# In-place low half of the residual on GpSimd, another order of SP's transfers, and the first norm and the clears moved, in a fused attention and feed-forward kernel

## The chip, the cores and the metric

One core of one Trainium2 chip. The metric is the device time of one execution in microseconds; it is given as the median of three runs. The core has five engines with instruction streams of their own, tied by semaphores: TensorE (PE), VectorE (DVE), ScalarE (ACT), GpSimd (POOL) and SyncE (SP), which here only issues DMA transfers.

## What is computed

A transformer layer on 2048 tokens of width 1024. The attention mixes the 32 heads of one token with each other (not tokens with tokens); the feed-forward weights are first quantized to 16 levels per block of 64 values and back.

```python
def reference(x, wq, bq, wk, bk, wv, bv, wl, bl, w1, w2, w3):
    x = x + attn(layernorm(x))
    x = x + ffn(layernorm(x))
    return x

def attn(h):                                  # heads H = 32, head width D = 32
    q, k, v = ((h @ w.T + b).reshape(B, S, H, D) for w, b in ...)
    scores = einsum("bshd,bstd->bsht", q, k) / sqrt(D)
    return einsum("bsht,bstd->bshd", softmax(scores), v).reshape(B, S, E)

def ffn(h):                                   # w1, w2: 2752 x 1024, w3: 1024 x 2752
    dq = nf4_quant_dequant                    # per block of 64: nearest of 16 levels times the block's absmax
    return (silu(h @ dq(w1).T) * (h @ dq(w2).T)) @ dq(w3).T
```

## The kernel before

Everything that PE multiplies in 16 bits is split into a high half (the value rounded to float16) and a low half (the rest), and the products are added.

**Stages.** The program first turns and splits the three projection weights (to about 64 us). Then comes the attention stage, 16 steps, one for each tile of 128 tokens: steps 0 and 1 are written out (`first_steps`), steps 2 to 13 are a loop of six passes with two steps each (u = 0, the even step, and u = 1), and steps 14 and 15 are written out. A short tail finishes the last two tiles while the first feed-forward weights are prepared. Then 11 rounds of feed-forward.

**One step n on PE** (`tensor.step`): the q projection of tile n (L1014), mixed with the scores of tile n-1 (L1051); the transposes of the normed tile n+1 (L285), which need DVE's norm L279; the k projection, mixed with the first half of the context products of tile n-1 (L1063), and the v projection with the second half. The context products need `p_diag`, written by ACT (L933).

**DVE in step n** (`vector.step`): evacuates projections (L752), takes norm statistics of tile n+1 (L261, L265, L267), applies the norm once POOL has the reciprocal root (L275), handles scores and softmax, and in between does four or five "looks" (L766): each takes block maxima of one tile of a feed-forward weight, which SP has loaded into one of two slots of `ff_raw`. A look waits for its load; a load waits until an earlier look has freed its slot.

**The second residual stream** (called with n-2): POOL adds the context to `x_res` (`residual`, L715); SP stores the sum as x1 (`store_x1`, L655); DVE takes its moments and normalizes `x_res` in place (L879) after that store; ACT writes the high half into `x2_half` (`halve2`, L981) and issues a DMA transpose of it to `x2_hi` (L609); POOL computes the low half into `x2_half` again (`low2`, L723), for which it waits until the high transpose has landed; ACT issues the transpose of it to `x2_lo` (L614) after `q_diag` (L933) is dispatched; SP stores both (`store_x2`, L661) and loads the next tile's residual into `x_res` (`load_res`, L256). In the tail SP issues the transposes itself. In the rows digits are left out of names: `x_half` is `x2_half`, `x_lo` is `x2_lo`, `x` as a target of L655 is x1.

**Order.** Each engine executes its stream in the order in which the step functions emit it, so SP, which waits on a semaphore before most transfers, holds back all transfers behind a wait. POOL clears `q_diag` and `p_diag` by one memset each in steps 0 and 1 (`clear`, L739).

## Time and profile before

| | us |
|---|---|
| median of 3 runs | 2000.74 |
| lowest and highest | 1997.92, 2001.58 |
| the profiled execution | 2001.23 |
| its span | 1999.5 |
| PE busy in the span | 1916.9 (96%) |
| DVE busy | 1740.5 (87%) |
| ACT busy | 1479.4 (74%) |
| POOL busy | 1192.9 (60%) |

The durations further down come from that one profiled execution, whose own time is 0.5 us above the median. Shares over the whole span mix stages: the attention stage fills about 64 to 580 us, the feed-forward rounds the rest. Times of a row are microseconds from the start of the span. Busy time of a matmul is modelled, so PE counts as busy where matmuls follow each other without a gap.

### The profile page before, as it was taken

What the parts mean: (1) busy time and instruction counts of PE and PEld (TensorE: products, weight loads), DVE (VectorE), ACT (ScalarE), POOL (GpSimd) and SP (SyncE); (2) the same over time, 40 slices, a digit from 0 to 9 for tenths busy, and PEclk for the clock granted to TensorE, in tenths of its full rate; (3) what the DMA queues carried; (4) which work ended last, traced back from release to release, by engine and by line L of the source; (5) the groups of instructions that cost most, each with busy time, mean ns of one, the idle gap of its engine ahead of it and who ended that gap; (6) DMA issues with size and microseconds to landing.
All of it is one profiled execution on the core that took longest, in us unless ns stands there. A gap on an engine that the chain in (4) does not pass through costs nothing. (4 is left out here: it accounts for less than half of the span.)

```text
span 1999.5 us, 31160 instructions
## 1 busy us (share of the span) xinstructions
PE 1916.9 (96%) x10444; PEld 1061.6 (53%) x10444; DVE 1740.5 (87%) x1853; ACT 1479.4 (74%) x1672; POOL 1192.9 (60%) x715
## 2 busy tenths in 40 slices
PE   6799999999988989999999999999999999999998
PEld 5487787777764334444444444444444444444443
DVE  6687878788777899999989999899998989999982
ACT  7234334352466889989989899898998989998883
POOL 0112121111143778787787977879778797786975
PEclk9899999999999999999999999999999999999999
DMA  9225554545345732221222212122121221212114
GB/s 305 95 85 147 161 165 131 183 129 178 108 169 132 231 91 53 53 54 42 56 50 48 57 42 62 44 53 53 42 63 43 57 49 42 63 42 59 38 27 180
DMA packets 253838, 184.06 MB, mean 92 GB/s; under 512 B 177840, under 2 KB 220848, under 8 KB 253744
## 3 DMA queue, kind: packets, MB, share of 16 engines
q1 hardware_dynamic: 224176, 175.67, 31.0%
q10 hardware_dynamic: 29568, 7.34, 1.9%
q8 instruction: 34, 0.56, 0.1%
q14 instruction: 60, 0.49, 0.1%
HBM read 115.34 MB, written 25.17 MB: 70 GB/s over the span
## 5 line engine op out<-in xcount | busy, mean ns | idle before, releaser
L1491 ACT ACTIVATE signs<-w_nat,compare_bias 128x1024 int8<-128x1024 f32 (+2 forms) x896 | 959.1, 1132 | 21.9 <-issue 14.5
L1627 DVE SCALAR_TENSOR_TENSOR bank<-signs,bank 128x1024 f32<-128x1024 int8 (+2 forms) x761 | 926.6, 1218 | 48.5 <-ACT signs L1491 20.8
L1798 PE MATMUL bank<-x2T_hi,w12T_hi 128*128 128x512 f16 x1376 | 522.6, 380 | 10.6 <-DMA w12T_lo<-half 6.4
L1800 PE MATMUL bank<-x2T_hi,w12T_lo 128*128 128x512 f16 x1376 | 522.5, 380 | 0.0
L1799 PE MATMUL bank<-x2T_lo,w12T_hi 128*128 128x512 f16 x1376 | 522.5, 380 | 0.0
L1014 PE MATMUL bank<-wT_hi,xT_hi 128*128 128x512 f16 x768 | 294.0, 383 | 2.4 <-PEq L325 2.4
L1014 PE MATMUL bank<-wT_hi,xT_lo 128*128 128x512 f16 x768 | 293.8, 383 | 0.0
L1825 PE MATMUL bank<-w3T_hi,hT_hi 128*128 128x512 f16 x672 | 255.7, 380 | 9.3 <-DMA w3T_lo<-half 3.8
L1827 PE MATMUL bank<-w3T_hi,hT_lo 128*128 128x512 f16 x672 | 255.6, 380 | 0.0
L1826 PE MATMUL bank<-w3T_lo,hT_hi 128*128 128x512 f16 x672 | 255.4, 380 | 0.0
L1417 POOL TENSOR_TENSOR acc<-acc,hidden 128x512 f32<-128x512 f32 x176 | 221.1, 1271 | 34.6 <-ACT hidden L1540 33.8
L1384 POOL TENSOR_SCALAR step_part<-w_nat 128x1024 f32<-128x1024 f32 (+1 forms) x64 | 230.5, 3602 | 14.3 <-POOL w_nat L1397 7.4
L1798 PEld LDWEIGHTS bank<-x2T_hi,w12T_hi 128*128 128x128 f16 x1376 | 134.6, 98 | 174.9 <-issue 6.4
L1800 PEld LDWEIGHTS bank<-x2T_hi,w12T_lo 128*128 128x128 f16 x1376 | 134.7, 98 | 162.8 <-issue 0.8
L1799 PEld LDWEIGHTS bank<-x2T_lo,w12T_hi 128*128 128x128 f16 x1376 | 134.7, 98 | 162.4 <-issue 0.8
L1393 POOL TENSOR_TENSOR w_nat<-w_nat,step_part 128x1024 f32<-128x1024 f32 (+1 forms) x64 | 149.8, 2340 | 101.6 <-DVE w_nat L1627 101.6
L966 ACT ACTIVATE probs<-probs 128x512 f32<-128x512 f32 x32 | 20.2, 631 | 238.3 <-DVE probs L873 238.0
L1540 ACT ACTIVATE hidden<-bank,un_scale 128x512 f32<-128x512 f32 x176 | 120.2, 683 | 91.5 <-PE bank L1827 36.1
L1063 PEld LDWEIGHTS bank<-vT,p_diag 128*128 128x128 f32 x1024 | 168.8, 191 | 22.4 <-ACT p_diag L933 7.8
L1051 PEld LDWEIGHTS bank<-kT,q_diag 128*128 128x128 f32 x1024 | 169.1, 191 | 14.6
L1063 PE MATMUL bank<-vT,p_diag 128*128 128x32 f32 x1024 | 155.9, 235 | 4.8 <-ACT p_diag L933 4.8
L1411 POOL TENSOR_TENSOR hT_lo<-hidden,hT_hi 128x512 f16<-128x512 f32 (+1 forms) x88 | 101.8, 1157 | 95.5 <-ACT hT_hi L1529 92.8
(143 smaller groups left out, 2613.7 us busy)
## 6 DMA issues: line engine op xcount, KB each, us to landing
ff_raw<-in_L_ffn_w SPq DMA_DIRECT2D x63, 512.0 KB, 5.1
w_nat<-in_L_ffn_w SPq DMA_DIRECT2D x63, 512.0 KB, 3.9
x_nat<-in_L_attn_hidden_states SPq DMA_DIRECT2D x16, 512.0 KB, 4.6
x_res<-in_L_attn_hidden_states SPq DMA_DIRECT2D x16, 512.0 KB, 4.0
x<-x_res SPq DMA_DIRECT2D x16, 512.0 KB, 3.1
acc<-x SPq DMA_DIRECT2D x4, 2048.0 KB, 8.5
out<-acc SPq DMA_DIRECT2D x16, 512.0 KB, 2.7
w_raw<-in_L_attn_wq SPq DMA_DIRECT2D x8, 512.0 KB, 7.4
```

The source lines that it names most:

```text
L1014: ins = nc.tensor.matmul(to, x, w, start=j == 0, stop=j == len(passes) - 1)
L1063: ins = nc.tensor.matmul(context[:, t], p_diag[:, t], vT[:, t // 2, :, t % 2], start=True, stop=True)
L1384: nc.gpsimd.tensor_scalar(step_part[0:rows, 0:cols], w_nat[0:rows, slot, 0:cols], float(BOUNDS[APART]), 2 * HALF_STEP[APART], ALU.is_gt, A ...
L1417: nc.gpsimd.tensor_tensor(acc[:, st, BANK:], acc[:, st, BANK:], hidden[:, st % 2], ALU.add).then_inc(summed, 1)
L1491: nc.scalar.activation(signs[0:rows, ring(v, k), 0:cols], w_nat[0:rows, v % SLOTS, 0:cols], ACT.Sign, scale=COMPARE[SUMMED[k]][0], bias=co ...
L1627: V.scalar_tensor_tensor(to, part, HALF_STEP[SUMMED[k]], before, ALU.mult, ALU.add).then_inc(sign_used, 1)
L1798: nc.tensor.matmul(dst, hi, x2T_hi[:, toks, c], start=c == 0, stop=False)
L1799: nc.tensor.matmul(dst, hi, x2T_lo[:, toks, c], start=False, stop=False)
L1800: last = nc.tensor.matmul(dst, lo, x2T_hi[:, toks, c], start=False, stop=c == C - 1)
L1825: nc.tensor.matmul(dst, hT_hi[k, p, toks], w3T_hi[k, p, cols], start=p == 0, stop=False)
L1826: nc.tensor.matmul(dst, hT_hi[k, p, toks], w3T_lo[k, p, cols], start=False, stop=False)
L1827: last = nc.tensor.matmul(dst, hT_lo[k, p, toks], w3T_hi[k, p, cols], start=False, stop=p == GROUP - 1)
```

## The change

Six edits:

1. `low2` writes the low half into the first half of `x_res`'s own bytes, seen as float16 (`x2_low`), instead of into `x2_half`. It waits for the high half (`x2_hi_done`), no longer for the high transpose. The low transpose reads `x2_low`.
2. ACT issues the low transpose before it places `q_diag`, no longer after.
3. SP's order within a step is another, and `load_res` waits for both transposes, since `x_res` now holds the low half until it is turned. In the tail SP issues the low transpose first and loads `x_res` when it has landed.
4. In the first step DVE takes the norm statistics before the first look, and applies the norm before the first evacuation and look.
5. POOL clears both `diag` tiles before the first step instead of in steps 0 and 1.
6. The first `load_res` and what stands behind it no longer wait for the first projection.

```diff
+        x2_low = x_res[:].bitcast(F16)[:, 0:E]
...
         def turn_low2(eng, n):
             eng.wait_ge(x2_lo_done, n + 1)
             eng.sem_inc(held, 1)
-            eng.dma_start_transpose(x2_lo[:], x2_half[:]).then_inc(x2_turned, 16)
+            eng.dma_start_transpose(x2_lo[:], x2_low).then_inc(x2_turned, 16)
...
                 todo = looks(n, u, it)
-                for look in todo[:1]:
+                for look in todo[:2]:
                     load_ff(*look)
                 if end:
                     store_x1(n - 2)
+                for look in todo[2:3]:
+                    load_ff(*look)
                 if normalize and not (it is None and n + 2 >= T):
                     sp.wait_ge(x_turned, 2 * n + 2)
                     load_x(sp, n + 2, u)
...
-                for look in todo[1:4]:
+                for look in todo[3:4]:
                     load_ff(*look)
                 if end:
                     sp.wait_ge(x2_turned, 32 * (n - 1))
-                    store_x2(n - 2)
+                    sp.sem_inc(held, 1)
+                for look in todo[4:]:
+                    load_ff(*look)
                 if end and attend:
                     load_res(sp, n - 1)
+                if end:
+                    store_x2(n - 2)
...
-                for look in todo[4:]:
-                    load_ff(*look)
...
                 turn_high2(sp, T - 2)
-                sp.wait_ge(x2_lo_done, T - 1)
+                turn_low2(sp, T - 2)
+                sp.wait_ge(x2_turned, 32 * (T - 1))
+                sp.sem_inc(held, 1)
                 load_res(sp, T - 1)
-                turn_low2(sp, T - 2)
                 store_x2(T - 2)
...
-            sp.wait_ge(projected, 1)
+            sp.wait_ge(w_turned, GROUPS * PAIRS)
             load_res(sp, 0)
...
             def low2(n):
-                pool.wait_ge(x2_turned, 32 * n + 16)
-                nc.gpsimd.tensor_tensor(x2_half[:], x_res[:], x2_half[:], ALU.subtract).then_inc(x2_lo_done, 1)
+                pool.wait_ge(x2_hi_done, n + 1)
+                nc.gpsimd.tensor_tensor(x2_low, x_res[:], x2_half[:], ALU.subtract).then_inc(x2_lo_done, 1)
...
+            pool.wait_ge(w_turned, GROUPS * PAIRS)
+            for diag in (q_diag, p_diag):
+                pool.memset(diag[:], 0.0).then_inc(diag_zero, 1)
             all_steps(pool, step, tail, feed)
...
                     turn_v(n)
-                look()
+                    look()
...
+                if normalize and not attend:
+                    norm_apply(dve, n + 1, 1 - u)
+                    look()
                 if project:
                     evacuate(n, u, it, 0, 0)
                 if attend:
                     center(n, 0)
-                if normalize:
+                if normalize and attend:
                     norm_apply(dve, n + 1, 1 - u)
...
                 if feed:
                     next(feed)
+                if end:
+                    turn_low2(act, n - 2)
                 if project:
                     act.wait_ge(q_ready, n + 1)
...
                     place(q_diag, qT[:].rearrange("p t h u -> p t u h"), q_placed)
-                if end:
-                    turn_low2(act, n - 2)
```

DVE at the start of the attention stage, before (`ff_raw` is the look's tile, `x_nat` the tile to be normed):

```order
L766 TENSOR_REDUCE absmax<-ff_raw 128x16 [waits bias_turned,ff_in0,bias_in,consts_set]
L261 BN_STATS stats<-x_nat 128x6 [waits x_in1]
L261 BN_STATS stats<-x_nat 128x6
L265 BN_AGGR mean_var<-stats 128x2 [waits dve_seq]
L267 TENSOR_SCALAR var_eps<-mean_var 128x1 [waits dve_seq]
L752 SCALAR_TENSOR_TENSOR qkv<-bank,scales,bias 128x512 [waits projected]
L279 TENSOR_SCALAR x_nat<-x_nat,mean_var,rstd 128x1024 [waits rstd_ready]
```

DVE at the same place now:

```order
L261 BN_STATS stats<-x_nat 128x6 [waits bias_turned,x_in1,bias_in,consts_set]
L261 BN_STATS stats<-x_nat 128x6
L265 BN_AGGR mean_var<-stats 128x2 [waits dve_seq]
L267 TENSOR_SCALAR var_eps<-mean_var 128x1 [waits dve_seq]
L279 TENSOR_SCALAR x_nat<-x_nat,mean_var,rstd 128x1024 [waits rstd_ready]
L769 TENSOR_REDUCE absmax<-ff_raw 128x16 [waits ff_in0]
L755 SCALAR_TENSOR_TENSOR qkv<-bank,scales,bias 128x512 [waits projected]
```

The first look moved from ahead of the statistics to behind the norm, and the norm from behind the first evacuation to ahead of it.

SP in the second half of the loop's even step, before, from the fourth look's load to the fifth's (a wait is named at the instruction behind it; the ISA and REGISTER_ALU rows prepare an address):

```order
L625 DMA ff_raw<-in_L_ffn_w 128x8x128
L643 REGISTER_ALU
L661 REGISTER_ALU [waits x2_turned]
L661 DMA x_hi_dram<-x_hi 128x1024
L661 DMA x_lo_dram<-x_lo 128x1024
L256 ISA
L256 DMA x_res<-in_L_attn_hidden_states 128x1024
L619 REGISTER_ALU
L623 ISA [waits absmax_done]
L623 DMA ff_raw<-in_L_ffn_w 128x1024
```

SP at the same place now:

```order
L626 DMA ff_raw<-in_L_ffn_w 128x8x128
L646 REGISTER_ALU
L620 REGISTER_ALU [waits x2_turned]
L624 ISA [waits absmax_done]
L624 DMA ff_raw<-in_L_ffn_w 128x1024
L256 ISA
L256 DMA x_res<-in_L_attn_hidden_states 128x1024
L666 REGISTER_ALU [waits x2_turned]
L666 DMA x_hi_dram<-x_hi 128x1024
L666 DMA x_lo_dram<-x_lo 128x1024
```

The fifth look's load moved ahead of the load of `x_res` and the two stores, and the load of `x_res` ahead of the stores.

SP in the tail, before, around the last load of `x_res`:

```order
L609 DMA_TRANSPOSE x_hi<-x_half 128x8x128 [waits x2_out,x2_hi_done]
L256 DMA x_res<-in_L_attn_hidden_states 128x1024 [waits x2_lo_done]
L614 DMA_TRANSPOSE x_lo<-x_half 128x8x128 [waits x2_lo_done]
L661 DMA x_hi_dram<-x_hi 128x1024 [waits x2_turned]
L661 DMA x_lo_dram<-x_lo 128x1024
```

SP at the same place now:

```order
L610 DMA_TRANSPOSE x_hi<-x_half 128x8x128 [waits x2_out,x2_hi_done]
L615 DMA_TRANSPOSE x_lo<-x_res 128x8x128 [waits x2_lo_done]
L256 DMA x_res<-in_L_attn_hidden_states 128x1024 [waits x2_turned]
L666 DMA x_hi_dram<-x_hi 128x1024 [waits x2_turned]
L666 DMA x_lo_dram<-x_lo 128x1024
```

The load of `x_res` moved behind the low transpose, and waits for it.

## Rows read from the trace of the kernel before

**Rows 1.** Table by stretches: busy us of PE, its weight loads, DVE, ACT, POOL.

```profile
1000.00:1500.00 500.00, 499.89 (x2315) 225.83 (x2313) 470.67 (x435) 451.48 (x492) 401.17 (x218) 1.00 0.22 51
```

**Rows 2.** Waits of PE, 60:130 us, then 130:600: total us, times, longest.

```profile
PE bank L285 <- DVE x_nat L279: 9.7, 1, 9.7
...
PE bank L285 <- DVE x_nat L279: 10.2, 7, 2.4
...
PE bank L1063 <- ACT p_diag L933: 4.8, 7, 0.8
```

**Rows 3.** Timelines at the start: start, duration, instruction, [idle before, what ended it].

```profile
71.06 0.37 SPq L623 DMA_DIRECT2D ff_raw<-in_L_ffn_w  x1
...
76.10 1.22 DVE L766 TENSOR_REDUCE absmax<-ff_raw 128x16 f32<-128x1024 f32 x1 [11.87 <-DMA ff_raw<-in_L_ffn_w]
...
79.64 3.52 POOL L739 MEMSET q_diag<- 128x4096 f32 x1
...
79.73 3.97 DVE L279 TENSOR_SCALAR x_nat<-x_nat,mean_var,rstd 128x1024 f32<-128x1024 f32 x1
...
83.76 1.97 PE L285 MATMUL bank<-ident,x_nat 128*128 128x128 f32 x8 [9.71 <-DVE x_nat L279]
```

**Rows 4.** Table by stretches: after the busy times granted clock, DMA share, GB/s.

```profile
84.00:89.00 5.00, 5.00 (x17) 2.73 (x17) 4.79 (x6) 1.93 (x3) 0.00 (x0) 0.50 0.34 107
```

**Rows 5.** Timelines of one odd step of the loop.

```profile
304.17 0.80 DVE L279 TENSOR_SCALAR x_nat<-x_nat,mean_var,rstd 128x1024 f32<-128x1024 f32 x1
...
305.02 1.09 PE L285 MATMUL bank<-ident,x_nat 128*128 128x128 f32 x8 [1.88 <-DVE x_nat L279]
...
311.04 1.04 ACT L981 ACTIVATE x_half<-x_res 128x1024 f16<-128x1024 f32 x1
...
315.32 2.13 POOL L723 TENSOR_TENSOR x_half<-x_res,x_half 128x1024 f16<-128x1024 f32 x1 [12.46 <-DMA x_hi<-x_half]
...
316.16 0.41 PE L1063 MATMUL bank<-vT,p_diag 128*128 128x32 f32 x2 [0.66 <-ACT p_diag L933]
...
317.57 1.25 ACTq L614 DMA_TRANSPOSE x_lo<-x_half  x1
318.44 2.29 ACT L933 ACTIVATE q_diag<-qT 32x1024 f32<-32x1024 f32 x2
...
325.41 0.75 DVE L752 SCALAR_TENSOR_TENSOR qkv<-bank,scales,bias 128x512 f32<-128x512 f32 x1 [0.96 <-PE bank L1014]
```

**Rows 6.** Timelines at the end of the even step that follows.

```profile
354.09 1.25 DVE L855 STREAM_TRANSPOSE flipped<-probs 128x1024 f32<-128x1024 f32 x1
358.63 1.22 DVE L766 TENSOR_REDUCE absmax<-ff_raw 128x1024 f32 x1 [3.29 <-DMA ff_raw<-in_L_ffn_w]
...
351.71 0.36 SPq L661 DMA_DIRECT2D x_hi_dram<-x_hi  x1
...
353.38 0.86 SPq L623 DMA_DIRECT2D ff_raw<-in_L_ffn_w  x2
```

**Rows 7.** Timelines of the tail and the opening of the feed-forward rounds.

```profile
625.93 0.33 SPq L256 DMA_DIRECT2D x_res<-in_L_attn_hidden_states  x1
...
630.72 0.35 SPq L661 DMA_DIRECT2D x_hi_dram<-x_hi  x1
...
632.69 0.59 SPq L655 DMA_DIRECT2D x<-x_res  x1
...
629.84 2.39 POOL L715 TENSOR_TENSOR x_res<-x_res,flipped 128x1024 f32<-128x1024 f32 x1 [2.08 <-DMA x_res<-in_L_attn_hidden_states]
...
642.08 0.81 DVE L879 TENSOR_SCALAR x_res<-x_res,mean_var,rstd 128x1024 f32<-128x1024 f32 x1 [6.83 <-DMA x<-x_res]
...
647.79 2.13 POOL L723 TENSOR_TENSOR x_half<-x_res,x_half 128x1024 f16<-128x1024 f32 x1 [12.95 <-DMA x_hi<-x_half]
...
654.24 1.06 ACT L1514 ACTIVATE half<-w_nat 128x1024 f16<-128x1024 f32 x1 [5.14 <-POOL w_nat L1397]
...
656.37 9.23 DVE L1627 SCALAR_TENSOR_TENSOR bank<-signs,bank 128x1024 f32<-128x1024 int8 x7 [2.56 <-ACT signs L1491]
```

More of the change, by code:

```diff
@@ L699, in step @@
                     inv_std(pool, n + 1)
-                if it is None:
-                    clear(n)
                 if end:
@@ L735, in tail @@
                 low2(T - 1)
-            def clear(n):
-                if n < 2:
-                    pool.memset((q_diag, p_diag)[n][:], 0.0).then_inc(diag_zero, 1)
+            pool.wait_ge(w_turned, GROUPS * PAIRS)
+            for diag in (q_diag, p_diag):
+                pool.memset(diag[:], 0.0).then_inc(diag_zero, 1)
             all_steps(pool, step, tail, feed)
```

## The prediction

> **What bounds the kernel now.** I read the table by stretches first. In the long feed-forward stretch TensorE (PE) is busy 499.9 of 500 us [rows 1]. Nothing of the change lies there, so whatever the attention stage gains or loses before about 740 us is passed on whole to the end. Next the waits of PE in the attention stage: one of 9.7 us at its start, seven of 10.2 us together for `x_nat` (L285), and seven of 4.8 us together for `p_diag` (L1063) [rows 2]. All of these are waits for VectorE (DVE) or for ScalarE (ACT) behind it. The timelines then say what held those engines. Reader, look at the square brackets: the idle time of the engine before the row, and what ended it.
>
> **Start of attention, the first norm ahead of the looks, the early clears.** DVE sat idle 11.87 us until `ff_raw` landed for the first look at 76.10; SP had issued that load only at 71.06, because it first waited for the first projection [rows 3]. The norm statistics of tile 1 stood behind that look although their data was there. Then the norm itself (L279) took 3.97 us, where the same instruction takes 0.80 later [rows 3, 5]: it ran beside the 3.52 us memset of GpSimd (POOL) and ended half a microsecond after it (79.64 + 3.52 = 83.16 against 83.70). PE had been ready at 83.76 - 9.71 = 74.05.
> In the changed order DVE starts with the statistics. The stage begins between 64.23 (76.10 - 11.87, where DVE was done with the stage before) and 65.3 (I take 64.4). POOL is the later one: two memsets, 7.0 us, then the reciprocal root, about 0.6 with its gap: 72.0, at latest 73.0. The norm's 0.80 ends at 72.9, at latest 73.8. Both are ahead of 74.05, so the whole wait goes: **9.7 us**. What is late next is PE itself, by a margin of 0.25 to 1.2 us.
> The gap also cost clock. After it PE ran 84 to 89 us at a granted clock of 0.50, that is at 1.2 instead of 2.4 GHz [rows 4]; from 83.76 to 89 that is 5.2 us of which half is lost, **2.6 us**. An idle of 1.88 us at 305 was followed by eight transposes in 1.09 us, where those after the long idle took 1.97 [rows 3, 5], so short waits do not bring this cost and only the long one does.
> The Trainium skill (SBUF — State Buffer, on the port pair shared by VectorE and GpSimd) calls the pair an exclusive lock for a whole instruction, taken by a VectorE instruction in a two-port mode. The trace agrees: 3.97 against 0.80 us. By this rule the statistics, with one input each, are not held up by the two memsets; if the small L267 were, it would still be free at the end of the first one, near 68, before POOL can use it.
>
> **SP's transfers by date; low half in place.** One step per token tile, two tiles per pass of the loop. In the odd step of a pass the norm starts at 304.17, PE had waited 1.88 us for it at 305.02, and it waits again 0.66 us for `p_diag` at 316.16 [rows 5]. Both hang on the same DVE chain, so the step loses 2.54 us. What made DVE late is at the end of the even step: its fifth look began 3.29 us late, waiting for `ff_raw` [rows 6]. DVE was through with `flipped` at 354.09 + 1.25 = 355.34, but SP issued that load (the first of the two at 353.38) behind the two stores of x2 and the load of `x_res`, and those stood behind the low transpose.
> Two edits bring it forward. First, the low half: ACT has written `x2_half` at 311.04 + 1.04 = 312.08, but POOL starts only at 315.32, when the high transpose has landed, and the low transpose is issued at 317.57, behind the dispatch of `q_diag` [rows 5]. Now POOL can run at 312.1 to 314.3. ACT's queue reaches the transpose when `p_diag` is nearly done, 314.8 to 316.1, so it goes out and lands 1.5 to 2.8 us earlier. Second, SP issues the fifth load directly after it instead of behind three other transfers (351.71 to 353.38, 1.7 us more). Together the load leaves 3.2 to 4.5 us earlier and lands, with the same 5.2 us of flight, at 354.1 to 355.4, as DVE gets there. Of the 3.29 us at most 0.1 stays; PE needs 2.54, so 0.65 us or more is spare. Both waits of PE go: 7 places, 10.2 + 4.8 = **15.0 us** [rows 2].
> What the edits cost there: the same transfers, the same POOL subtraction (2.13 us, nobody waits for POOL at 312). ACT now issues the low transpose (1.25 us of its queue) ahead of `q_diag`, which can begin up to 1.3 us later. It ended at 318.44 + 2.29 = 320.73; PE starts the next tile about 325.4 (DVE's row at 325.41 follows PE's last product) [rows 5], so 4.7 us of cover become 3.4. SP waits for x_res's store (residual) before the third look's load and the next `x_nat`; these are used 7 and 30 us later. The residual add itself may start earlier, since `x_res` is loaded ahead of the stores. I cost all of this at nothing.
>
> **Change to the tail.** The load of the last `x_res` was issued at 625.93, as soon as POOL had read it. Now the low half lives in `x_res`, so the load waits until the low transpose has landed, which was seen at 630.72 [rows 7]; without the load beside it I take 630. The last residual moves from 629.84 to about 634, and the store of x1 from 632.69 to about 637. That store, not the add, holds DVE: it landed when norm L879 could start at 642.08, 9.4 us after its issue, because token loads of 2 MB stood in front. They still do. Two halves of x2, 2 MB of tokens and this store, 3 MB, passed between 630.72 and 642.08, 0.26 MB/us. The 0.5 MB of `x_res` that now travel ahead in the same stretch make 1.9 us, less 0.7 for the stretch's earlier start: +1.2 us.
> Against it: POOL's last low half waited 12.95 us until 647.79 for the high transpose. Now it follows the half at 644 and frees POOL 2.6 us sooner, after which ACT's wait of 5.14 us (ended at 654.24) and the 2.56 us of DVE at 656.37 fall away [rows 7]. The chain of quantized weights through DVE sets PE's waits up to 740 us, so the tail gives 2.6 - 1.2 = **1.4 us**. Ends of this term: 3 us of cost, if the store lands 3 us later and nothing is given back, and 4 us of gain, if the store keeps its date and later waits of PE shrink too.
> The Trainium skill (DMA: Bandwidth & Descriptors, Queues, rings and completion order) says each DMA engine takes the descriptors of a ring in order. The 9.4 us of a 512 KB store agree. By this rule alone 512 KB put ahead are a loss of their whole passage, 1.9 in place of 1.2 us, and the sum is 0.7 us worse.
>
> **Sum.** 9.7 + 2.6 + 15.0 + 1.4 = 28.7 us. The profiled execution took 2001.2 us (its span 1999.5, and 1.7 around it), 0.5 above the median 2000.7. So 1972.5 for an execution like it, and **1972.0** as a median.
>
> **Rivals.**
> (a) The loop's wait is only passed on. If PE finds another limit in place of `x_nat` (the fifth load lands late in the burst of four transfers that now leave together, or `p_diag` keeps its own date), half or all of the 15 us stays. For it: the two waits of a step come in a row, and DMA is crowded there. Against: the even steps have the same chain and no wait at all, with DVE 3.3 us better off. Times: 1979.5 with half, 1987 with all.
> (b) The tail costs. The last x_res load is late, the 2.56 us are not given back and the store lands 3 us later: 1.4 + 3 = 4.4 us more, 1976.4.
> (c) Slower. GpSimd's in-place write of a 16-bit tile over the 32-bit one that it reads is a form that no row has. The nearest (L723, in place in 16 bits) takes 2.13 us. If it took D us, `q_diag` would end at 312.1 + D + 1.25 + 4.6, and PE's scores wait from D = 7.5 us on, 14 times. The gain of 28.7 us is used up 2.05 us further, at D = 9.5. At D = 10.5 it costs 14 x 3 = 42 us: 2014. Nothing speaks for a factor of five.
> (d) The change does not do what it says at the start: POOL's memsets begin late and the norm misses 74.05. Up to 2 us are lost, without a fall of the clock: 1974, inside the forecast's own spread.
>
> **Chances.** Forecast with (d): 0.62. (a): half 0.11, all 0.07. (b): 0.13. (c) 0.03, and 0.04 for a result within 0.2% by several of these at once. A measurement of this kernel tells about 0.2%, 4 us, from no change. Faster by more: 0.93; within: 0.04; slower: 0.03. The range reaches down to 1966.5 (the tail's 4 us instead of 1.4, and 3 more if DVE's shorter waits bring PE forward elsewhere too) and up to 1983, which takes in (b), half of (a) and both at once; about 0.15 is left out.
>
> **What would show it.** In the profile after: the wait before the first L285 of the attention stage under 1 us, L279 there near 0.8 us, and no stretch at clock 0.50 near 84 us. The seven waits for `x_nat` and seven for `p_diag` gone, and DVE's wait for `ff_raw`, now up to 3.29 us at a time, under 0.5 us in the loop. POOL's low half right behind ACT's half. In the tail, norm L879 0 to 2 us later against its neighbours, POOL's last low half at once. Wrong it would be if PE waits in the loop under another name, or if the last `x_res` moves PE's first waits in the feed-forward part by more than 3 us.

## The result and the profile after

| | before | after |
|---|---|---|
| median, us | 1999.99 | 1967.39 |
| lowest and highest, us | 1997.92, 2001.58 | 1964.42, 1968.27 |
| span of the profiled execution, us | 1999.5 | 1966.5 |

The ratio of after to before is 0.9835, 95% interval 0.9818 to 0.9852. By the medians the kernel is 32.6 us faster, by the spans 33.0; the forecast was 28.7. The median of before is 1999.99 and not 2000.74, because a fourth run of it was taken beside the changed kernel. Of the runs further down, one of the eight executions of e9_slow1 took 6561.78 us and is left out of that kernel's ratio. In the code of after most line numbers are 2 to 6 higher (L1014 is L1020, L1063 is L1069, L879 is L885, L723 is L727, L766 is L769), and the in-place low half shows as `x_res<-x_res,x_half` in the rows.

The start of attention, timelines of all engines, in the columns of [rows 3]:

```profile
68.12 3.51 POOL L743 MEMSET p_diag<- 128x4096 f32 x1
71.60 0.56 POOL L275 TENSOR_TENSOR rstd<-var_eps,power 128x1 f32<-128x1 f32 x1
72.20 0.81 DVE L279 TENSOR_SCALAR x_nat<-x_nat,mean_var,rstd 128x1024 f32<-128x1024 f32 x1 [5.38 <-POOL rstd L275]
...
74.05 1.04 PE L285 MATMUL bank<-ident,x_nat 128*128 128x128 f32 x8
```

The norm ends at 73.01 and PE does not wait. The row of the table by stretches that answers to [rows 4]:

```profile
84.00:89.00 5.00, 5.00 (x26) 2.38 (x25) 2.10 (x4) 0.00 (x0) 0.00 (x0) 1.00 0.39 105
```

The granted clock is 1.00 where it was 0.50, and PE runs 26 instructions in the 5 us where it ran 17. The waits of PE in 130:600 us, all there are (against the lower two of [rows 2]; the 9.0 us stood there in the trace of before too):

```profile
PE bank L1861 <- issue: 9.0, 1, 9.0
PE bank L1804 <- DVE w_nat L1650: 2.6, 1, 2.6
PE bank L1861 <- ACT hT_lo L1508: 0.9, 1, 0.9
```

**Where the 33.0 us lie.** The first transposes of `x_nat` of each step (L285) are good dates, since each step has them once. Three of before, then three of after:

```profile
143.22 1.07 PE L285 MATMUL bank<-ident,x_nat 128*128 128x128 f32 x8
...
176.40 1.09 PE L285 MATMUL bank<-ident,x_nat 128*128 128x128 f32 x8 [2.38 <-DVE x_nat L279]
...
208.00 1.07 PE L285 MATMUL bank<-ident,x_nat 128*128 128x128 f32 x8
```

```profile
130.78 1.07 PE L285 MATMUL bank<-ident,x_nat 128*128 128x128 f32 x8
...
161.43 1.07 PE L285 MATMUL bank<-ident,x_nat 128*128 128x128 f32 x8
...
192.07 1.07 PE L285 MATMUL bank<-ident,x_nat 128*128 128x128 f32 x8
```

Behind a first one of 30.64 us the period was 32.0 to 33.2 us in one step and 31.6 (32.0 in the last) in the next, in turn; it is 30.64 in every step now. Summed up from such dates:

| stretch | before | after | gain | forecast |
|---|---|---|---|---|
| wait before the first L285 | 9.71 | 0 | 9.7 | 9.7 |
| first to second L285 | 28.82 | 26.09 | 2.7 | 2.6 |
| second to last L285 (13 steps) | 416.12 | 398.36 | 17.8 | 15.0, with the next line |
| last L285 to the first L1855 (now L1861) | 59.40 | 58.16 | 1.2 | |
| behind it, to the end | | | 1.6 | 1.4 |

Of the 4.3 us that came beyond the forecast, 4.0 are the loop's (17.8 and 1.2 against 15.0).

### The profile page after: what moved, and what is told of

Its sections match the earlier page's. It is cut to its first block and busy times, and to the rows that moved or that the text cites. A ratio compares the mean times of both kernels' runs of the same rounds, so it can differ in the third digit from the quotient of the medians.

```text
span 1966.5 us, 31163 instructions
## 1 busy us (share of the span) xinstructions
PE 1910.7 (97%) x10444; PEld 1060.9 (54%) x10444; DVE 1734.3 (88%) x1853; ACT 1479.7 (75%) x1672; POOL 1193.6 (61%) x715
## 5 line engine op out<-in xcount | busy, mean ns | idle before, releaser
L1804 PE MATMUL bank<-x2T_hi,w12T_hi 128*128 128x512 f16 x1376 | 522.2, 379 | 8.1 <-DMA w12T_lo<-half 5.5
L1020 PE MATMUL bank<-wT_hi,xT_hi 128*128 128x512 f16 x768 | 292.6, 381 | 2.4 <-PEq L325 2.4
L1020 PE MATMUL bank<-wT_hi,xT_lo 128*128 128x512 f16 x768 | 292.6, 381 | 0.0
L1804 PEld LDWEIGHTS bank<-x2T_hi,w12T_hi 128*128 128x128 f16 x1376 | 134.8, 98 | 172.0 <-issue 4.2
L972 ACT ACTIVATE probs<-probs 128x512 f32<-128x512 f32 x32 | 20.2, 630 | 217.7 <-DVE probs L879 217.3
L1069 PEld LDWEIGHTS bank<-vT,p_diag 128*128 128x128 f32 x1024 | 169.0, 191 | 14.8
L1410 POOL TENSOR_TENSOR half<-w_nat,half 128x1024 f16<-128x1024 f32 (+1 forms) x66 | 139.8, 2118 | 31.9 <-ACT half L1520 31.9
```

The costliest lines, as they stand in the source:

```text
L1020: ins = nc.tensor.matmul(to, x, w, start=j == 0, stop=j == len(passes) - 1)
L1804: nc.tensor.matmul(dst, hi, x2T_hi[:, toks, c], start=c == 0, stop=False)
```

## A wait costs more than its row says

Here is why, in rows of before around one wait for `p_diag` in an odd step (first fence) and at the same place in the even step that follows (second):

```profile
186.13 0.38 PE L1014 MATMUL bank<-wT_hi,xT_lo 128*128 128x512 f16 x1
186.35 0.30 PE L1063 MATMUL bank<-vT,p_diag 128*128 128x32 f32 x2
186.49 0.38 PE L1014 MATMUL bank<-wT_hi,xT_hi 128*128 128x512 f16 x1
187.54 0.41 PE L1063 MATMUL bank<-vT,p_diag 128*128 128x32 f32 x2 [0.67 <-ACT p_diag L933]
187.78 0.38 PE L1014 MATMUL bank<-wT_hi,xT_lo 128*128 128x512 f16 x1
```

```profile
218.07 0.38 PE L1014 MATMUL bank<-wT_hi,xT_hi 128*128 128x512 f16 x1
218.43 0.41 PE L1063 MATMUL bank<-vT,p_diag 128*128 128x32 f32 x2
218.67 0.38 PE L1014 MATMUL bank<-wT_hi,xT_lo 128*128 128x512 f16 x1
```

Without a wait L1063 starts 0.22 us behind L1014 (186.13 to 186.35), although L1014's row lasts 0.38: matmuls overlap. At the wait it starts 1.05 behind (186.49 to 187.54), and the next L1014 follows after 0.24 in place of 0.14. The step loses 0.83 + 0.10 = 0.93 us where the bracket says 0.67, for the bracket counts from the modelled end of the product before. In the even step there is no bracket at all, and still 0.36 in place of 0.22 and 0.24 in place of 0.14: 0.24 us lost. Such a stall without a row stands in three of the six even steps (at 218.43, 282.52 and 347.06: 0.24, 0.18 and 0.24 us); at 155 us and in the last two there is none. For L285 the same correction is 0.15 us (33.18 - 30.64 = 2.54 for a bracket of 2.38 and no other wait). So: 10.2 + 7 x 0.15 for L285, 4.8 + 7 x 0.27 for `p_diag` in odd steps, and 0.7 in the three even ones: 18.6 us by an estimate from these rows, against 19.0 measured.

## The experiments

Each ratio is taken against runs of the kernel before on the same chip, so the ratios compare better than the medians. "Step 1" is first to second L285, "13 steps" second to last.

| kernel | median | ratio and interval | step 1 | 13 steps |
|---|---|---|---|---|
| after | 1967.39 | 0.9835 (0.9818 to 0.9852) | 26.09 | 398.36 |
| e1_start_only | 1986.45 | 0.9942 (0.9927 to 0.9957) | 26.10 | 413.47 |
| e2_no_start | 1978.69 | 0.9908 (0.9894 to 0.9921) | 28.82 | 398.36 |
| e3_sp_old | 1966.18 | 0.9840 (0.9826 to 0.9853) | 26.10 | 398.36 |
| e4_low_old | 1985.10 | 0.9936 (0.9922 to 0.9949) | 26.10 | 414.19 |
| e5_act_old | 1964.72 | 0.9837 (0.9819 to 0.9854) | 26.09 | 398.37 |
| e6_clears_old | 1965.97 | 0.9845 (0.9828 to 0.9862) | 26.10 | 398.36 |
| e7_tail_low | 1966.17 | 0.9844 (0.9828 to 0.9860) | 26.15 | 398.36 |
| e8_memset1 | 1971.10, 1 run | | 27.83 | 398.36 |
| e8_memset2 | 1975.93, 1 run | | 28.18 | 398.36 |
| e9_slow1 | 1993.79 | 0.9980 (0.9969 to 0.9992) | 26.16 | 417.33 |
| e9_slow2 | 2047.86 | 1.0248 (1.0231 to 1.0265) | 26.10 | 456.09 |
| e10_slow_half | 1982.31 | 0.9922 (0.9906 to 0.9939) | 26.16 | 405.95 |

**Start and loop apart (e1, e2).** e1 is the kernel before with the edits at the start alone:

```diff
-            sp.wait_ge(projected, 1)
+            sp.wait_ge(w_turned, GROUPS * PAIRS)
...
+            for diag in (q_diag, p_diag):
+                pool.memset(diag[:], 0.0).then_inc(diag_zero, 1)
...
+                if normalize and not attend:
+                    norm_apply(dve, n + 1, 1 - u)
+                    look()
```

> The kernel before with the edits at the start alone: first norm ahead of the looks, both clears first, SP's early wait. Loop, low half and tail stay as before. Comparing the two traces, TensorE reached the first feed-forward matmul 31.4 us earlier, of which I had forecast 27.3. Theory A (the start gives what its rows say: a wait of 9.7 us and 2.7 us of halved clock): 12.4 us faster than before, about 1987.6, and the seven waits for x_nat and seven for p_diag stay at 10.2 and 4.8 us. Rival B (the 4 us that came beyond the forecast belong to the start, since everything behind it begins better placed): 16.5 us faster, about 1983.5. Rival C (loop waits grow when the loop starts earlier against SP's loads): under 10 us faster, above 1990.

e2 is the changed kernel with this same diff taken back.

> The changed kernel with the start as before: first look ahead of the statistics, clears in steps 0 and 1, SP behind the first projection. Theory A: the loop's edits are worth 19.0 us and not the 15.0 of the rows, because a wait in a row is counted from the modelled end of the product before it, while the products are issued closer than they last (0.14 to 0.22 us apart with 0.30 to 0.38 in the row), and because waits of 0.2 us in the even steps have no row. With 1.5 to 2 us of the tail: 12.4 us slower than the changed kernel, about 1979.8, the wait of 9.7 us and a stretch at clock 0.50 back, and no wait of TensorE in the loop. Rival B (the extra 4 us are the start's): 1983.5.

Waits of PE in 130:600 us, e1 and then e2:

```profile
PE bank L1855 <- issue: 8.3, 1, 8.3
PE bank L285 <- DVE x_nat L279: 8.2, 6, 1.5
PE bank L1063 <- ACT p_diag L933: 4.8, 7, 0.8
```

```profile
PE bank L1861 <- issue: 7.4, 1, 7.4
PE bank L1861 <- ACT hT_lo L1508: 0.9, 1, 0.9
```

e2 has 398.36 us in its 13 steps: the loop's gain of 17.8 us does not need the start. Its wait of 9.7 us and its step 1 of 28.82 us are back. That bears out theory A in the trace: 12.4 us are the start's, 19.0 the loop's. The medians are too wide to add to it (against the changed kernel's ratio, e2 is 14.6 us slower where 12.4 were expected, and e1 gains 11.6 us over before, each good to some 3 us). One thing was not expected: in e1 the loop's 13 steps shrank too, from 416.12 to 413.47, for which I followed no cause. With the loop's own edits in place these 2.65 us are part of the 17.8.

**Which edit makes the loop's gain (e3, e4, e5).** e3 puts SP's order within the step back:

```diff
-                for look in todo[:2]:
+                for look in todo[:1]:
...
-                for look in todo[3:4]:
+                for look in todo[1:4]:
                     load_ff(*look)
                 if end:
                     sp.wait_ge(x2_turned, 32 * (n - 1))
-                    sp.sem_inc(held, 1)
-                for look in todo[4:]:
-                    load_ff(*look)
+                    store_x2(n - 2)
                 if end and attend:
                     load_res(sp, n - 1)
-                if end:
-                    store_x2(n - 2)
...
+                for look in todo[4:]:
+                    load_ff(*look)
```

> The changed kernel with SP's order in the step as before: the fifth look's load behind the stores of x2 and the load of x_res. Low half in place, ACT's order and the start stay changed. As the prediction reads it, the early low half alone brings the load 1.5 to 2.8 us forward, VectorE was 3.29 us late, and TensorE feels it from 0.75 us of lateness: 0 to 1.0 us in each of 7 passes, so 1967 to 1974.5. Rival (from the trace of the changed kernel, where the fifth load leaves at 325.62 and lands some 3 us before its look at 333.03, and the norm behind it ends 1.8 us before TensorE wants it): behind three more transfers it still comes in time, no wait in the loop at all, 1967.4 within 0.1%.

e4 keeps SP's new order and takes back the date of the low half and ACT's order:

```diff
-                pool.wait_ge(x2_hi_done, n + 1)
+                pool.wait_ge(x2_turned, 32 * n + 16)
...
-                if end:
-                    turn_low2(act, n - 2)
                 if project:
...
                     place(q_diag, qT[:].rearrange("p t h u -> p t u h"), q_placed)
+                if end:
+                    turn_low2(act, n - 2)
```

> The changed kernel in which GpSimd's low half waits for the high transpose again and ACT issues the low transpose behind q_diag, as before. SP's new order and the start stay. As the prediction reads it, SP's order alone brings the fifth load 1.7 us forward of the 3.29 us that it was late: 1.6 us stay at VectorE, 0.85 us at TensorE, in 7 passes 6 us, about 1973.5, with L279 and p_diag waits named in the loop. Rival (slack of 4.8 us in the changed kernel against 4 us of delay): no wait of TensorE in the loop, 1967.4 within 0.1%, and the low half in place is then not needed beside SP's order.

e5 has only the second half of that diff.

> The changed kernel, with ACT issuing the low transpose behind q_diag again; GpSimd's low half stays in place and without the wait for the high transpose. With both undone (e4) the loop's 15 us of waits were back, so this run says which of the two carries the gain. Theory A (the low half's date carries it): ACT's queue reaches the transpose some 3 us later than the 291.6 of the changed kernel's step, against a slack of 4.8 us, so no wait of TensorE in the loop, period of a step 30.64 us, 1967 within 0.1%. Rival (ACT's order carries it): the transpose leaves behind q_diag whatever GpSimd does, VectorE waits 1 to 2 us for the fifth look, and half of the 19 us is back, about 1976.

e3 and e5 cannot be told from the changed kernel, to 0.01 us in the 13 steps and within the intervals in the medians. e4 is 20.2 us slower than the changed kernel by the ratios (17.1 by the spans), and no better than e1. Its waits in 130:600 us, PE's and the one of DVE's that matters:

```profile
PE bank L1069 <- ACT p_diag L939: 7.5, 12, 0.8
...
PE bank L285 <- DVE x_nat L279: 4.3, 7, 1.8
```

```profile
DVE absmax L769 <- DMA ff_raw<-in_L_ffn_w: 24.3, 15, 3.2
```

PE's waits are spread over more steps and most are smaller, but the 13 steps take as long as in e1. The trace says why SP's order did not help. In e1 it is above all the fifth look of the even steps that waits for its load, 2.9 to 3.3 us at a time. In e4 that wait is 0.8 us or less, but now the first look of the next step waits, 1.2 to 3.2 us in every step: its load stands behind that of `x_res` and the two stores of x2.

```profile
154.49 1.22 DVE L769 TENSOR_REDUCE absmax<-ff_raw 128x1024 f32 x1 [2.51 <-DMA ff_raw<-in_L_ffn_w]
```

So SP's order by itself brought nothing (414.19 us against 413.47 with the old one), and ACT's by itself is not needed (e5). With GpSimd's low half in place and without the wait for the high transpose, either of them can be undone at no cost. That edit carries the loop's gain as far as these runs go. Two combinations were not run: the low half alone, with the old orders of both SP and ACT, and the old wait with ACT's new order. Both rivals of e4's expectation fell: I had 6 us and nothing, it was 20.

**How much room the low half has (e9, e10).** The prediction priced a slow low half as rival (c): D is the time from ACT's half to GpSimd's, and nothing should happen below 7.5 us. e9 puts a multiplication of `x_res` by 1.0 ahead of the subtraction, with a reciprocal root that repeats `rstd2` (the values stay the same), once or twice; e10 only the root, four times:

```diff
+                nc.gpsimd.tensor_tensor(rstd2[:], var_eps2[:], power[:, 0:1], ALU.pow).then_inc(more, 1)
+                nc.gpsimd.tensor_scalar(x_res[:], x_res[:], 1.0, None, ALU.mult).then_inc(more, 1)
+                pool.wait_ge(more, n * 2 + 2)
                 nc.gpsimd.tensor_tensor(x2_low, x_res[:], x2_half[:], ALU.subtract).then_inc(x2_lo_done, 1)
```

> The changed kernel with a slower low half: GpSimd also multiplies x_res by 1.0 in place and takes the reciprocal root once more in between, so that the low half is ready about 6.6 us after ACT's half (D, 2.1 in the changed kernel). The prediction's rival (c) says that TensorE feels nothing below D = 7.5 us: 1967 within 0.1%. Rival reading: the fifth look's load waits for the low transpose and has 4.8 us of slack, which D = 6.6 nearly uses: 0 to 1 us in each of 7 passes, up to 1974.

> The same with the multiplication and the root twice: D about 11.1 us. By the prediction's rival (c), whose limit is q_diag's date for the scores of TensorE: 14 x (11.1 - 7.5) = 50 us slower than the changed kernel, 2017. By the date of q_diag in the trace of the changed kernel (scores start at 303.44, q_diag could start at 289.38 + D + 1.25 and takes 4.6): limit D = 8.2, 14 x 2.9 = 41 us, 2008. By the fifth look alone (limit D = 7.0, 7 passes): 29 us, 1996.

D is 2.2 us in the changed kernel. It came out at 5.6 us in e9_slow1 (the half ends at 297.25, the low half at 302.84), and this cost 29 us by the ratios (25.7 by the spans), all of the loop's gain and more. In e9_slow2 it came out at 9.0 us, not 11.1, and cost 83 us. Each of my limits was too generous. e10 was then to find the limit:

> The changed kernel with the reciprocal root taken four more times ahead of the low half: ready about 4.6 us after ACT's half in place of 2.1, so that the low transpose is issued about 10.1 us after TensorE's transposes of x_nat. That distance is 7.6 us in the changed kernel, 8.8 with ACT's old order (no cost), 12.8 with one multiplication more (27 us slower), 12.6 before the change. Theory A: everything that SP issues next stands behind the landing of this transpose, the next step's first look above all; its load had 5.2 us more delay than in the changed kernel and VectorE waited 2.1 us for it, so 3.1 us were spare, and a transpose up to 10.7 us behind costs nothing: 1967 within 0.1%, no wait of TensorE in the loop. Rival (the cost grows evenly from the date of the changed kernel or of ACT's old order): 8 to 13 us slower, 1975 to 1980.

Theory A fell again: e10 is 17 us slower than the changed kernel by the ratios and 12.6 by the spans (1979.1 against 1966.5), 7.6 of them in the 13 steps. The first disturbed step shows which transfer is the tight one. SP's queue and DVE in e10, then the same two places after:

```profile
143.92 0.33 SPq L625 DMA_DIRECT2D ff_raw<-in_L_ffn_w  x1
...
146.07 0.35 SPq L625 DMA_DIRECT2D ff_raw<-in_L_ffn_w  x1
...
153.93 1.22 DVE L778 TENSOR_REDUCE absmax<-ff_raw 128x1024 f32 x1 [1.99 <-DMA ff_raw<-in_L_ffn_w]
```

```profile
143.91 0.35 SPq L624 DMA_DIRECT2D ff_raw<-in_L_ffn_w  x1
...
152.21 1.18 DVE L769 TENSOR_REDUCE absmax<-ff_raw 128x1024 f32 x1
```

Behind the landing of the low transpose SP issues five transfers in a row, 2 MB: the fifth look's load, `x_res`, two stores of x2, and the first look's load of the next step. In e10 the last of them was issued at 146.07 and landed 7.7 us later, at 153.8; DVE had been ready 1.8 us before. In the changed kernel the same load was issued at 143.91 and landed 6.2 us later, at 150.1, and DVE took it at 152.21: 2.1 us to spare. Over the 13 steps the first look's load has 1.8 to 2.8 us to spare; e10's expectation had worked out 3.1 from the waits of e9_slow1. In e5, whose low transpose leaves 8.8 us behind L285, the same load landed at 151.7 and DVE took it at 151.87: 0.1 us to spare, at no cost. In e10 the transfer also took 1.5 us longer than in the changed kernel, and the next load (issued at 150.22) went out while it was still on its way; that the one slowed the other is not shown.

This also explains e3: the order among the five hardly changes when the fifth of them lands (at 150.5 in e3, whose first L285 comes 1.0 us later than in the changed kernel). But the old order leaves less room. The smallest that any look has in the 13 steps is 0.2 us in e3 and 1.8 us in the changed kernel.

From there the lateness feeds itself. DVE is late, so its norm of `x_res`, ACT's half and the transpose come later in the next step: ACT's half starts 4.3 us behind L285 in the changed kernel (288.26 against 284.00) and 5.8 in e10 (292.47 against 286.67), the low transpose leaves 11.7 behind L285 where 10.1 had been put in. Before the change it was 12.55 [rows 5], now 7.61. That e5 with 8.8 costs nothing and e10 with 10.1 does, places the limit between them, and by e5's 0.1 us close to e5.

Of e10's 12.6 us by the spans, 7.6 are in the 13 steps, 3.1 more in PE's wait ahead of the first feed-forward matmul (12.1 us against 9.0), 1.1 elsewhere between the last L285 and that matmul, and 1.2 behind it; the start gave 0.4 back. What set the parts outside the 13 steps is open.

**The start: clears and clock (e6, e8).** e6 puts the clears back behind the reciprocal root in steps 0 and 1:

```diff
-            for diag in (q_diag, p_diag):
-                pool.memset(diag[:], 0.0).then_inc(diag_zero, 1)
...
+                if it is None:
+                    clear(n)
```

> The changed kernel with GpSimd's two clears back in steps 0 and 1, behind the reciprocal root. The prediction let the norm wait for two memsets (7.0 us) and end at 72.9. Theory A: with the statistics first the root is done near 68.5, the norm then runs beside the memset and takes about 3.9 us again, to about 72.7, still before TensorE wants it at 74.05; the second memset has 3 us of cover in step 1. No wait, 1967 within 0.1%, and the early clears are worth nothing by themselves. Rival: norm and memset in step 1 delay the second norm past TensorE's date of 100.14 by up to 3 us: about 1970.

```profile
66.28 0.56 POOL L275 TENSOR_TENSOR rstd<-var_eps,power 128x1 f32<-128x1 f32 x1 [14.74 <-DVE var_eps L267]
66.78 3.52 POOL L745 MEMSET q_diag<- 128x4096 f32 x1
66.87 3.97 DVE L279 TENSOR_SCALAR x_nat<-x_nat,mean_var,rstd 128x1024 f32<-128x1024 f32 x1 [0.68 <-POOL rstd L275]
```

The norm took its 3.97 us beside the memset again, and ended at 70.84, still 2.6 us ahead of PE's L285 at 73.43 (in the changed kernel 1.0 us ahead). Theory A holds: the early clears bring nothing. That leaves the order of DVE (edit 4) and SP's earlier loads (edit 6), which no run parts. The trace speaks for DVE's order: statistics and norm wait for no transfer of this stretch, and the norm ends at 73.01 whatever `ff_raw` does. But the first look now stands ahead of the first evacuation, and its load was issued at 65.10 where before it was 71.06 [rows 3]; whether the 12.4 us need edit 6 as well is not shown. e8 puts one or two more memsets (3.5 us each) ahead of the two, to let PE idle for a time that I set:

```diff
+            for k in range(1):
+                pool.memset(q_diag[:], 0.0).then_inc(more, 1)
+                pool.wait_ge(more, k + 1)
             for diag in (q_diag, p_diag):
```

> The changed kernel with one more memset of q_diag (3.5 us) ahead of the two. The first norm then ends at about 76.5 and TensorE, ready at 74.05, idles 2.5 us. Theory A: as after the idles of 1.2 to 2.4 us in the loop before the change, the clock does not fall: the step behind it keeps its 26.1 us from first to second transposes of x_nat, and the cost is the wait alone. Rival: any idle at the start costs clock, the step is over 27 us.

> The same with two more memsets (7.0 us): TensorE idles about 6.0 us. The 9.7 us of before brought a granted clock of 0.50 for 5 us and a step of 28.8 in place of 26.1 us. Theory A: an idle of 6 us does the same, full price: 6.0 + 2.7 us. Rival A2: the price comes only with the longer idle, 6.0 us alone and a step of 26.1. Rival A3: in between, a clock partly lower, a price that grows with the idle.

L285 in e8_memset1, and in e8_memset2:

```profile
76.26 1.92 PE L285 MATMUL bank<-ident,x_nat 128*128 128x128 f32 x8 [2.40 <-DVE x_nat L279]
```

```profile
81.10 1.97 PE L285 MATMUL bank<-ident,x_nat 128*128 128x128 f32 x8 [5.09 <-DVE x_nat L279]
```

After an idle of 2.40 us the eight transposes took 1.92 us, against 1.04 without, and step 1 took 27.83 us, 1.7 longer. After 5.09 us it was 2.1 longer, after 9.71 us 2.7 [rows 3]. The granted clock accounts for all three. It was 0.50 from 76.4 to 79.8 us in e8_memset1, from 78.4 to 85.3 in e8_memset2 and from 79.0 to 89.2 before the change. Of these stretches 3.4, 4.2 and 5.4 us lie behind the start of L285 (76.26, 81.10, 83.76), and half of that was lost: 1.7, 2.1 and 2.7 us. So in these three the price is half of what is left of the slow stretch when PE resumes, and it rises less than the idle does. e8_memset2 went by A3. Each of the two is a single run.

Theory A of e8_memset1 is wrong, and with it a sentence of the prediction: an idle of 2.38 us at 176.40 in the kernel before cost no clock (its period is explained above to the last 0.15 us), one of 2.40 us at the start did. Nor does the loop protect from it. e9_slow2, whose steps have several waits each, fell to 0.50 for 3.4 us five times in its 13 steps. Two of its L285, after a wait of 1.76 us and after one of 3.14:

```profile
450.24 1.96 PE L285 MATMUL bank<-ident,x_nat 128*128 128x128 f32 x8 [1.76 <-DVE x_nat L279]
...
557.96 1.09 PE L285 MATMUL bank<-ident,x_nat 128*128 128x128 f32 x8 [3.14 <-DVE x_nat L279]
```

The shorter wait had the transposes run at half speed, the longer one did not. The length of the last idle alone does not tell, and neither does the place; what does is not shown by these runs.

**The tail (e7).** The low half of tile 14 goes to a free tile, so that `x_res` is loaded as early as before the change:

```diff
+        tail_low = ff_raw[:, 1].bitcast(F16)[:, 0:E]
...
-                turn_low2(sp, T - 2)
-                sp.wait_ge(x2_turned, 32 * (T - 1))
-                sp.sem_inc(held, 1)
+                sp.wait_ge(x2_lo_done, T - 1)
                 load_res(sp, T - 1)
+                turn_low2(sp, T - 2, tail_low)
```

> The changed kernel with the low half of tile 14 alone (the one of the tail) written into the second slot of ff_raw, whose last look is over, and transposed from there. x_res is free as soon as GpSimd has read it, and SP issues its last load ahead of the low transpose, as before the change: about 595.1 where the changed kernel issues it at 598.25. Theory A (what the trace of the changed kernel shows: the norm L885 behind the store of x1 came only 0.4 us late against TensorE's dates): nothing that a median can tell, the norm at most 0.4 us earlier, 1967. Rival (the prediction's term of 1.2 us, or its end of 3 us): norm and all behind it 1.2 to 3 us earlier, 1964.4 to 1966.2.

The changed kernel in the tail, then e7; the matmul row is a date common to both:

```profile
598.25 0.34 SPq L256 DMA_DIRECT2D x_res<-in_L_attn_hidden_states  x1
599.35 0.39 PE L1804 MATMUL bank<-x2T_hi,w12T_hi 128*128 128x512 f16 x1 [2.63 <-DVE w_nat L1650]
...
604.93 0.36 SPq L660 DMA_DIRECT2D x<-x_res  x1
...
611.00 0.81 DVE L885 TENSOR_SCALAR x_res<-x_res,mean_var,rstd 128x1024 f32<-128x1024 f32 x1 [3.08 <-DMA x<-x_res]
...
612.98 2.13 POOL L727 TENSOR_TENSOR x_res<-x_res,x_half 128x1024 f16<-128x1024 f32 x1 [5.47 <-ACT x_half L987]
```

```profile
593.01 0.33 SPq L256 DMA_DIRECT2D x_res<-in_L_attn_hidden_states  x1
...
597.32 0.39 PE L1804 MATMUL bank<-x2T_hi,w12T_hi 128*128 128x512 f16 x1 [2.63 <-DVE w_nat L1650]
...
599.82 0.57 SPq L661 DMA_DIRECT2D x<-x_res  x1
609.55 0.81 DVE L885 TENSOR_SCALAR x_res<-x_res,mean_var,rstd 128x1024 f32<-128x1024 f32 x1 [7.18 <-DMA x<-x_res]
```

Against L1804 e7 issues the load of `x_res` 3.2 us earlier and the store of x1 3.1 us earlier, and the norm still starts 0.6 us later (12.23 behind L1804 against 11.65). The store took 9.6 us to land in e7 and 6.0 in the changed kernel: what it gains in date it spends behind the token load issued ahead of it (`x2T_lo`, L1340). In both kernels it landed 1.3 to 1.4 us behind that load, and in the kernel before too, so the norm's date went with the token load and not with the store's own issue. Theory A holds in the main (the norm came 0.6 us later, where at most 0.4 earlier was expected), and the medians agree.

No kernel of these beats the changed one by more than its interval.

## Why the prediction was right, point by point

- **Total.** 1972.0 was forecast, 1967.4 measured, 4.6 us less and inside the range, but only 0.9 us above its lower end. The range reached so far down for a gain of 4 us in the tail and for shorter waits elsewhere. What used it up was mostly neither: the loop's waits were read too short. To that extent it was luck. The direction, the mechanism at the start and the waits that go in the loop hold.
- **First norm.** Forecast: POOL is the later one, L279 ends at 72.9. Measured 73.01. The wait of 9.7 us is gone whole.
- **Clock.** 2.6 us forecast, 2.7 measured (28.82 against 26.09). The size was right, as it was read from the slow stretch itself. The sentence that short waits do not bring this cost was wrong: 2.40 us brought 1.7 us of it (e8_memset1).
- **Early clears.** I let the gain rest on them without asking what the norm would do beside a memset at its new date. e6 shows that it is in time either way; they cost nothing and brought nothing.
- **Loop, 15.0 us.** Mis-sized: 19.0. The rows understate a wait by 0.15 and 0.27 us, and the sentence "the even steps have the same chain and no wait at all" missed 0.18 to 0.24 us in three of the six, which has no bracket. The size of DVE's own wait was read from one pass too: 3.29 us was not the longest, at 165.87 it was 4.18.
- **Loop, the two edits.** This step failed in its working. The low transpose was to land 1.5 to 2.8 us earlier and SP's order to bring 1.7 us more, and the two were added up against the 2.54 us. The low half does it with SP's old order (e3), and SP's order without the low half does nothing (e4): it moved the fifth look's load forward and left the next step's first load behind the others. The transpose now leaves 4.9 us earlier against L285 (12.55 to 7.61). 1.8 of these are lateness that had fed itself (ACT's half started 6.02 behind L285 [rows 5], now 4.26), 3.2 the edit.
- **`q_diag` later at no cost.** Holds: scores of PE show no wait for it.
- **Tail, 1.4 us.** 1.6 measured, by two errors that cancel only in part. The norm L885 came 0.4 us late against the first feed-forward matmul, not 1.2: it starts right behind the store, and the store landed right behind the token load ahead of it, whatever its own date (e7). PE's waits behind it shrank from 1.54, 3.24 and 3.19 us to none, 2.48 and 3.03, together 2.5 us, as the 2.6 had been read; 0.9 us of it was lost again. 0.55 lie between the first feed-forward matmul and the wait of 0.9 us behind it (27.08 us before, 27.63 after), and they are clock: behind that matmul the granted clock was 0.50 for 2.9 us before and for 4.0 after, and half of the difference is lost. The rest, along the rounds, is not explained.
- **Rivals.** (a) and (b) did not come. (c) had the right place and a wrong price: the limit is not 7.5 us of D, by `q_diag`, but under 4.7 (e10), by the first look's load at the end of SP's row of transfers. GpSimd's in-place write takes 2.13 us as before, and that alone kept (c) away. Had the low half come at D = 5.6 us, the kernel would have been nearly as slow as before (e9_slow1, 0.9980).

## What to carry to other kernels

Ask of an edit not only which wait it removes but by how much the new date is in time, at the last transfer of the burst that hangs on it, not at the first: here that transfer had 2 us to spare and not the 3 to 5 that I had worked out, and a low half 2.5 us later used them up. Read its landing in the trace of the kernel itself. A new order of transfers can buy room and no time: SP's left 1.8 us in place of 0.2, and no run here needed them. The wait in a row of overlapping matmuls was too small here each time (0.67 for 0.93 us, 2.38 for 2.54), and dates of one line from step to step give the true loss, small unnamed stalls included. When several edits come together, undo them one at a time: of six here, the low half without its wait carries the loop, and the edits of the start other than the clears carry the start; between DVE's order and SP's earlier loads these runs do not decide.

## What the runs showed that was not expected

- PE's idle of 2.40 us at the start cost 1.7 us of clock, 5.09 us cost 2.1 and 9.71 us 2.7. In the loop 2.38 us cost none before the change, but in e9_slow2 a wait of 1.76 us was followed by transposes at half speed and one of 3.14 us was not.
- A low half that came 2.5 us later on GpSimd cost 17 us, 3.4 us later cost 29 us: past the limit the loop loses in most steps, since the lateness comes round again through ACT's half.
- PE's wait ahead of the first feed-forward matmul, for which the profile names nothing, differs between kernels that are alike up to it: 9.0 us in the changed kernel, 7.6, 7.2, 7.9 and 7.2 in e3, e5, e6 and e7. That is of the size of the differences between their medians (1964.7 to 1967.4). It was 12.1, 12.0 and 16.0 us in e10, e9_slow1 and e9_slow2, whose loops are late; what sets it stays open.
